# A Perceiver block on one Trainium2 core: the third norm's variance from sums, a second ring of split chunks, GpSimd without arithmetic behind attention, four loads issued earlier

## The chip, the cores and the metric

The kernel runs on one core of one Trainium2 chip, in float32, with 256 query tokens and 25088 context rows of width 2048. The metric is the device time of one execution in microseconds (us); lower is better. The kernel before was timed in three runs: 2530.39, 2532.25 and 2534.62 us, so the median is 2532.25 us.

## The reference

Three residual sub-blocks are computed. x is 256 x 2048, ctx is 25088 x 2048.

```
x = x + softmax(LN(x) @ ctx.T) @ ctx                         # cross attention over 25088 rows
q,k,v = LN(x) @ Wq, Wk, Wv + biases                          # 32 query heads, 8 key/value heads, DH 64
x = x + attention over the HEADS axis of each token          # scores[d,e] = sum_h q[d,h] k[e,h]
y = LN(x)
x = x + y @ W_base.T + b_base + sum_e route_e * (y @ A_e.T) @ B_e.T    # 8 experts, rank 16, top 2
```

In the second sub-block k and v are repeated four times along the head axis, so its output o, 256 x 2048 after the reshape, consists of 512 different columns, each four times in a row. LN is (x - mean) / sqrt(var + 1e-5) over the 2048 columns, without weights.

## The kernel before, in words

**Float32 by splitting.** A float32 product a*b runs on TensorE (PE) as three products of rounded halves (`product`, L1384 to L1386): hi*hi, hi*lo and lo*hi. The hi part is a cast on ScalarE (ACT), the lo part a subtraction of the hi part, on VectorE (DVE) or GpSimd (POOL).

**The long loop (up to 2200 us)** goes over 49 blocks of 512 context rows. The change leaves it alone. Behind it the k, q and v projections run on PE until 2304.8 us.

**Weights of the last product.** During the long loop W_base was turned into `wt_dram`, 64 pieces of 128 x 512 (4 output blocks `ob` times 16 input chunks), and its fourfold column sums into `wp_dram`, 16 such pieces (4 output blocks times 4 chunks). A piece is a "chunk" w, numbered 0 to 79: 0 to 63 multiply the x from before the second sub-block (`xt_hi`, `xt_lo`), 64 to 79 multiply the 512 columns of o. Since the third norm is linear once mean and variance are known, the kernel works out base(x1) and base(o) apart and scales both by ln3_a = 1/std at the end.

**The road of one chunk.** POOL issues its load into one of 4 buffers of `tr` (`load_base`, L636 to L648; it first waits until chunk w-4 is split). ACT casts it to `ch_hi` (`hi_base`, L836 to L840; it waits for the load and until PE has used chunk w-4, since `ch_hi` and `ch_lo` have 4 buffers too). The lo part is made on DVE (`lo_base`, L1193 to L1196) or on POOL (`lo_base`, L650 to L653): `by_pool(w)` gives POOL every fourth chunk below 64 and every second one from 64 on. Then PE does 6 matmuls of 512 columns (3 products for each of 2 token tiles). Every engine works strictly in the order in which the program lists its work, so whatever stands ahead of a wait delays what stands behind it.

**Chunks 0 to 15** run on PE behind the v projection, with small groups of transposes between (`A_AFTER`, `GATE_AFTER`, `SUM_AFTER`, `GSUM_AFTER`, `V_AFTER`). On ACT the drain of such a group stands behind the cast of the chunk four further on. Chunks 0 to 3 are loaded early (L656), but on POOL chunk 3's split and the loads from chunk 4 on stand behind `pool.wait_ge(qkv_done, 3 * TT)` at L682, which is the end of the v projection, and behind three memsets of `v_t`. Meanwhile the SP queue stores the split queries (`qk_dram`), reads them back in another layout (`q_t`, 12 transfers) and loads the broadcast bias `b_base_all` (1 MB).

**Attention** is a loop of 16 steps (`o`) on all engines, three chunks a step: scores (L1551), maximum and subtraction on DVE (L1229, L1233), exponent on ACT (L881), transposes on PE (L1412), the product with v (L1605). `keep_base` (ACT L848, DVE L1205) saves an output block's PSUM into `base_x` after every 16th chunk.

**Behind attention (from 2452 us).** PE does `router_chunks` (16 chunks of 136 columns, x1 times expert A and gate), in three parts, 0 to 6, 6 to 12 and 12 to 16. Between the last two it transposes the normalised attention output; ACT writes it as `o_nat` with its sums, DVE centres it (`oc_nat`), PE transposes that (`G_OC`), and PE multiplies it with the router's column sums (the "sum products") and with chunks 64 to 79 (`sum_chunks(ob)`, 24 matmuls each). DVE has one list of work here: `x2_tile(t)` adds o to x1 in `acc` (L1298), `x2_variance(t)` takes its statistics (L1303), ACT takes the root (`deviation`, L729), `factors` makes ln3_a (L995 to L999), then come the router's logits, softmax, top 2 and `hw` (up to L1351), with splits of chunks in between. `hw` is transposed on PE (L1686), copied by ACT (L959), and `experts_out(ob)` (L1677, a full float32 matmul of 2 passes) closes each output block. PE's order is sum_chunks 0, 1, 2, the transposes of hw, experts_out 0, sum_chunks 3, experts_out 1, 2, 3. POOL meanwhile splits half of the chunks and adds the bias to x2 in 8 pieces of 128 x 512 (`X2B_AFTER`, L700). At the end DVE adds `base_x` (`with_base`, L1362) and the PSUM sums (`result`, L1369), 8 passes each, and SP stores the 8 output pieces.

```
            for w in range(RING_TR, ALL_W + 3):
                if w < ALL_W:
                    load_base(w)
                if by_pool(w - 3):
                    lo_base(w - 3)
```

## Time and profile before

| what | value |
|---|---|
| median of three runs | 2532.25 us (2530.39 to 2534.62) |
| the profiled execution's own time | 2524.54 us |
| its span in the profile | 2522.9 us |
| busy PE, DVE, POOL, ACT | 2453.0, 1954.9, 1431.9, 1093.3 us |
| mean granted TensorE clock | 0.993 of full |

Busy times are sums over the span; a busy PE is not one at its peak, since its matmuls overlap in the records. Times such as "2482.91" are us from the start of the span. The timeline gives start, duration, engine, line, operation and, in brackets, how long the engine sat idle before it and what released it. The chain that ended last follows each piece of work back to what released it.

### The profile page before, as it was taken

The numbers are of one execution on the slowest core, as the hardware profiler recorded it, in microseconds if no ns is written. First come the engines' busy times: TensorE is split into PE (matmuls) and PEld (weight loads), VectorE is DVE, ScalarE is ACT, GpSimd is POOL, SyncE is SP. The second block draws the span as 40 slices with busy tenths as digits, with TensorE's granted clock in tenths as the row PEclk, the third lists the DMA queues.
The fourth block names the chain that finished last, engine by engine and source line by source line (L and its number), as shares of the span: only waits on it lengthen the run. The fifth ranks groups of instructions, "written<-read, shape, count | busy, mean of one in ns | idle before, by whom it ended". The sixth has DMA issues, their size and how long they took to land.

```text
span 2522.9 us, 36094 instructions
## 1 busy us (share of the span) xinstructions
PE 2453.0 (97%) x11446; PEld 2007.1 (80%) x11446; DVE 1954.9 (77%) x2693; ACT 1093.3 (43%) x1576; POOL 1431.9 (57%) x1064
## 2 busy tenths in 40 slices
PE   5999999999999999999999999999999999998997
PEld 4788888888888888888888888888888888876775
...
GB/s 236 216 224 206 228 207 231 219 204 226 207 229 226 211 216 212 218 219 209 222 217 202 219 218 220 213 218 212 205 219 220 217 215 211 213 160 145 146 112 67
DMA packets 421111, 518.22 MB, mean 205 GB/s; under 512 B 54406, under 2 KB 296070, under 8 KB 418440
## 3 DMA queue, kind: packets, MB, share of 16 engines
...
## 4 chain that ended last, share of the span: by engine, by line
PE 92%; DVE 4%; DMA 2%; SPq 1%; ACT 1%; issue 1%; POOL 0%; DVEq 0%; ACTq 0%; POOLq 0%
PE ps L1384 30%; PE ps L1386 30%; PE ps L1385 30%; PE ps L1393 2%; DMA tr<-wt_dram 1%; DVE ch_lo L1031 1%; DMA raw<-in_ctx_dram 1%; SPq L406 1%; DVE top_f L1339 0%; PE ps L1605 0%; PE ps L1551 0%; PE ps L1412 0%; DVE tr L1027 0%; DVE acc L1151 0%; PE ps L1677 0%
## 5 line engine op out<-in xcount | busy, mean ns | idle before, releaser
L585 POOL TENSOR_TENSOR nat_lo<-raw,nat_hi 128x512 fp32r<-128x512 f32 x784 | 1170.5, 1523 | 874.6 <-ACT nat_hi L738 842.1
L1031 DVE TENSOR_TENSOR ch_lo<-tr,ch_hi 128x512 fp32r<-128x512 f32 x784 | 849.9, 1084 | 369.0 <-ACT ch_hi L727 368.9
L727 ACT CAST ch_hi<-tr 128x512 fp32r<-128x512 f32 x784 | 477.2, 621 | 808.1 <-PE ps L1386 800.1
L1384 PE MATMUL ps<-ch_hi,xt_hi 128*128 128x512 f32 x1696 | 677.5, 399 | 14.9 <-DVE ch_lo L1031 9.9
L1386 PE MATMUL ps<-ch_hi,xt_lo 128*128 128x512 f32 x1696 | 663.3, 391 | 0.0
L1385 PE MATMUL ps<-ch_lo,xt_hi 128*128 128x512 f32 x1696 | 662.1, 390 | 0.0
L1384 PE MATMUL ps<-nat_hi,pt_hi 128*128 128x512 f32 x1568 | 611.8, 390 | 3.7 <-DVE pt_lo L980 3.7
L1386 PE MATMUL ps<-nat_hi,pt_lo 128*128 128x512 f32 x1568 | 610.3, 389 | 0.0
L1385 PE MATMUL ps<-nat_lo,pt_hi 128*128 128x512 f32 x1568 | 610.1, 389 | 0.0
L1027 DVE STREAM_TRANSPOSE tr<-quart 128x512 f32<-128x512 f32 x784 | 546.8, 698 | 0.0
L738 ACT CAST nat_hi<-raw 128x2048 fp32r<-128x2048 f32 x196 | 374.5, 1911 | 208.9 <-PE ps L1386 194.4
L1384 PEld LDWEIGHTS ps<-ch_hi,xt_hi 128*128 128x128 f32 x1696 | 319.3, 188 | 83.4 <-DVE ch_lo L1031 11.4
L1386 PEld LDWEIGHTS ps<-ch_hi,xt_lo 128*128 128x128 f32 x1696 | 319.0, 188 | 68.5
L1385 PEld LDWEIGHTS ps<-ch_lo,xt_hi 128*128 128x128 f32 x1696 | 319.6, 188 | 61.7
L1384 PEld LDWEIGHTS ps<-nat_hi,pt_hi 128*128 128x128 f32 x1568 | 294.3, 188 | 69.0 <-DVE pt_lo L980 4.4
L1386 PEld LDWEIGHTS ps<-nat_hi,pt_lo 128*128 128x128 f32 x1568 | 294.4, 188 | 61.4
L1385 PEld LDWEIGHTS ps<-nat_lo,pt_hi 128*128 128x128 f32 x1568 | 294.4, 188 | 60.7
L1069 DVE SCALAR_TENSOR_TENSOR acc<-acc,alpha,ps 128x512 f32<-128x512 f32 x248 | 177.7, 716 | 26.7 <-PE ps L1386 25.7
L711 ACT CAST pt_hi<-ps 128x512 fp32r<-128x512 f32 x98 | 57.2, 585 | 120.3 <-PE ps L1393 120.3
L1078 DVE SCALAR_TENSOR_TENSOR acc<-acc,alpha,ps 128x512 f32<-128x512 f32 x144 | 101.1, 702 | 4.9 <-PE ps L1386 4.9
L744 ACT ACTIVATE probs<-ps,neg_max 128x512 f32<-128x512 f32 x98 | 67.2, 686 | 77.5 <-DVE neg_max L1051 77.5
L1196 DVE TENSOR_TENSOR ch_lo<-tr,ch_hi 128x512 fp32r<-128x512 f32 x56 | 39.3, 710 | 71.9 <-ACT ch_hi L840 71.2
...
## 6 DMA issues: line engine op xcount, KB each, us to landing
...
```

The costliest lines, as they stand in the source:

```text
L585: last = pool.tensor_tensor(nat_lo[:, j, t], raw[:, j % 2, t], nat_hi[:, j, t].bitcast(F32), ALU.subtract)
L711: act.copy(dst, src).then_inc(hi_drained, 1)
L727: act.copy(ch_hi[:, c % RING_CH, :], tr[:, c % RING_TR, :]).then_inc(chunk_hi, 1)
L738: act.copy(nat_hi[:, j], raw[:, j % 2]).then_inc(nat_hi_ready, 1)
L744: act.activation(probs[:, q, :], ps[:, SCORE_BANK + TT * new + q, :], ACT.Exp, bias=neg_max[:, new, q:q + 1], accum_out=row_sum[:, q:q + 1 ...
L1027: dve.transpose(tr[:, c % RING_TR, :].rearrange("p (r i) -> p r i", i=SQ), src).then_inc(chunk_transposed, 1)
L1031: dve.tensor_tensor(ch_lo[:, c % RING_CH, :], tr[:, c % RING_TR, :], ch_hi[:, c % RING_CH, :].bitcast(F32), ALU.subtract).then_inc(chunk_s ...
L1069: dve.scalar_tensor_tensor(piece, piece, alpha[:, 1 - turn.parity, q:q + 1], ps[:, out_bank(v, turn.over), :], ALU.mult, ALU.add).then_inc ...
L1078: dve.scalar_tensor_tensor(piece, piece, alpha[:, turn.parity, q:q + 1], ps[:, out_bank(v, False), :], ALU.mult, ALU.add).then_inc(acc_upd ...
L1384: pe.matmul(out_, a_hi, b_hi, start=start, stop=False)
L1385: pe.matmul(out_, a_hi, b_lo, start=False, stop=False)
L1386: return pe.matmul(out_, a_lo, b_hi, start=False, stop=stop)
```

## The change

**Loads sooner.** POOL splits chunk 3 and issues loads 4 to 7 right behind the column sums of the expert weights, ahead of the wait for the v projection and the memsets.

**POOL's arithmetic behind attention is gone.** `by_pool(w)` is now only for chunks below 64, so DVE splits all of 64 to 79. The 8 bias additions move into the attention stage: one behind each of loads 22, 26, ... 50, and they add the bias to x1 (`acc` before o is added) into `x2_b`. DVE adds o later, into `x2_b`.

**Variance from sums.** With o repeated four times, var(x1 + o) = var(x1) + (2 * cross + square) / 2048, where cross = sum over 512 columns of (fourfold sum of x1 - 4 mean) * o and square = 4 * sum of (o - mean o)^2. DVE makes the fourfold sums of x1 (`x1_sum`, one `tensor_reduce` of 128 x 2048 to 128 x 512 a tile) in attention steps 10 and 11, and behind attention four `scalar_tensor_tensor` passes of 128 x 512 with an accumulated result, and two small ones. The second addition of 128 x 2048 a tile, its 8 `bn_stats` and 2 `bn_aggr` are no longer ahead of the factors; the additions themselves come behind `hw`.

**A second ring.** x1 (`acc`) isn't needed once bias additions and x1_sum are done. Its 16 KiB become `more_hi` and `more_lo`, 4 buffers each. Chunks 68 to 71 and 76 to 79 use them, so that from chunk 68 on a cast waits for chunk w-8 instead of w-4. ACT casts 68 to 71 and DVE splits them right at the end of attention, on DVE ahead of `att_norm(1)`.

**Orders.** PE: `router_chunks` in parts 0 to 4, 4 to 8, 8 to 14 (behind the transposes of attention's output) and 14 to 16 (behind the G_OC groups); sum_chunks 0, 1, 2, transposes of hw, experts_out 0 and 1, sum_chunks 3, experts_out 2 and 3. DVE and ACT: as in the diff.

```
     STEP_W = 3
+    MORE_W = BASE_W + RING_CH
     assert OCT * STEP_W == BASE_W - PRE_W
...
     def by_pool(w):
-        return w % 4 == 3 if w < BASE_W else w % 2 == 1
+        return w < BASE_W and w % 4 == 3
+    def users_before(w):
+        return w + 1 - (RING_CH if w < MORE_W else 2 * RING_CH)
...
         stages = (stage, sb("stage_b", [P, 4 * P]))
-        b_nat = sb("b_nat", [P, DC, ER])
-        acc = sb("acc", [P, TT, DIM])
+        at_b = room(8 * KIB)
+        b_nat = put(at_b, "b_nat", [P, DC, ER])
+        x1_sum = put(at_b, "x1_sum", [P, TT, QKC])
+        scrap = put(at_b + 4 * KIB, "scrap", [P, TT, QKC])
+        at_acc = room(16 * KIB)
+        acc = put(at_acc, "acc", [P, TT, DIM])
+        more_hi = put(at_acc, "more_hi", [P, RING_CH, KB], F32R)
+        more_lo = put(at_acc + 8 * KIB, "more_lo", [P, RING_CH, KB], F32R)
         xt_hi = sb("xt_hi", [P, DC, TOK], F32R)
...
         att_t = put(at_lo, "att_t", [P, 4, 4, P])
+        scrap2 = put(at_lo, "scrap2", [P, TT, QKC])
         o_norm = put(at_lo + 8 * KIB, "o_norm", [P, KVH, P])
...
                 pool.wait_ge(chunk_hi, DC * NB + w + 1)
-                pool.tensor_tensor(ch_lo[:, w % RING_CH, :], tr[:, w % RING_TR, :], ch_hi[:, w % RING_CH, :].bitcast(F32),
+                pool.tensor_tensor(w_lo(w), tr[:, w % RING_TR, :], w_hi(w).bitcast(F32),
                                    ALU.subtract).then_inc(pool_split, 1)
...
+            lo_base(3)
+            for w in range(RING_TR, 2 * RING_TR):
+                load_base(w)
             pool.wait_ge(qkv_done, 3 * TT)
...
             pool.wait_ge(v_zeroed, 3)
-            for w in range(RING_TR, ALL_W + 3):
-                if w < ALL_W:
-                    load_base(w)
+            def add_bias(piece):
+                t, cols = piece // FB, slice(piece % FB * KB, (piece % FB + 1) * KB)
+                if piece == 0:
+                    pool.wait_ge(bias_loaded, 4 * 16)
+                    pool.wait_ge(group_done, G_GSUM + 1)
+                pool.tensor_tensor(x2_b[:, t, cols], acc[:, t, cols], b_base_all[:, cols], ALU.add).then_inc(x1b_ready, 1)
+            for w in range(2 * RING_TR, ALL_W):
+                load_base(w)
                 if by_pool(w - 3):
                     lo_base(w - 3)
-                for piece in X2B_AFTER.get(w - 3 - BASE_W, ()):
-                    t, ob = piece // FB, piece % FB
-                    cols = slice(ob * KB, (ob + 1) * KB)
-                    if ob == 0:
-                        pool.wait_ge(x2_ready, t + 1)
-                    if piece == 0:
-                        pool.wait_ge(bias_loaded, 4 * 16)
-                    pool.tensor_tensor(x2_b[:, t, cols], acc[:, t, cols], b_base_all[:, cols], ALU.add).then_inc(x2b_ready, 1)
+                if w in BIAS_AFTER:
+                    add_bias(BIAS_AFTER[w])
...
                 act.wait_ge(base_loaded[w % RING_TR], 16 * (w // RING_TR + 1))
-                act.wait_ge(chunk_used, DC * NB + w + 1 - RING_CH)
-                act.copy(ch_hi[:, w % RING_CH, :], tr[:, w % RING_TR, :]).then_inc(chunk_hi, 1)
+                act.wait_ge(chunk_used, DC * NB + users_before(w))
+                if w == MORE_W:
+                    act.wait_ge(x1b_ready, TT * FB)
+                    act.wait_ge(x1_summed, TT)
+                act.copy(w_hi(w), tr[:, w % RING_TR, :]).then_inc(chunk_hi, 1)
...
             act.activation(warm[:, 0:1], ones[:, 0:1], ACT.Sqrt)
+            for w in range(MORE_W, MORE_W + RING_CH):
+                hi_base(w)
...
                 act.activation(router_x[:, t, :], ps[:, t, 0:AG], ACT.Copy, scale=ln_b[:, t:t + 1]).then_inc(router_kept, 1)
-            def base_range(first, end_):
-                for w in range(BASE_W + first, BASE_W + end_):
-                    hi_base(w)
-            base_range(RING_CH, STD_AT)
             for t in range(TT):
...
             act.activation(warm[:, 1:2], ones[:, 0:1], ACT.Exp)
-            base_range(STD_AT, EXP_AT)
+            for w in range(MORE_W + RING_CH, MORE_W + RING_CH + EXP_AT):
+                hi_base(w)
             for t in range(TT):
...
                                accum_out=gate_s[:, t:t + 1]).then_inc(gate_exped, 1)
-            base_range(EXP_AT, FB * PC)
+            for w in range(MORE_W + RING_CH + EXP_AT, ALL_W):
+                hi_base(w)
             act.wait_ge(hwt_done, 1)
...
                     att_norm(0)
+                if o in SUM_AT:
+                    if o == SUM_AT[0]:
+                        dve.wait_ge(plain_done, H_B + DC // 4)
+                        dve.tensor_scalar(mean4[:, :], mean_var[:, :, 0], float(REP), None, ALU.mult)
+                    t = SUM_AT.index(o)
+                    dve.tensor_reduce(x1_sum[:, t, :], acc[:, t, :].rearrange("p (n j) -> p n j", j=REP), AX.X,
+                                      ALU.add).then_inc(x1_summed, 1)
+            for w in range(MORE_W, MORE_W + RING_CH):
+                lo_base(w)
             att_norm(1)
...
                                   o_mean[:, t:t + 1], None, ALU.subtract).then_inc(oc_ready, 1)
-            for t in range(TT):
+            def lo_oc(t):
                 lo_group(G_OC + t, oc_lo[:, :, t * P:(t + 1) * P], bank4(PLAIN_BANK + t), oc_hi[:, :, t * P:(t + 1) * P])
-            def x2_tile(t):
-                dst = acc[:, t, :].rearrange("p (n j) -> p n j", j=REP)
-                link(dve.tensor_tensor(dst, dst, o_nat[:, t, :].unsqueeze(2).broadcast_to([P, QKC, REP]), ALU.add))
-                dve.sem_inc(x2_ready, 1)
-            def x2_variance(t):
-                for i in range(4):
-                    last = dve.bn_stats(stats[:, t, i, :], acc[:, t, i * 512:(i + 1) * 512])
-                link(last)
-                variance(t)
+            dve.wait_ge(x1_summed, TT)
+            for t in range(TT):
+                dve.scalar_tensor_tensor(scrap[:, t], x1_sum[:, t], mean4[:, t:t + 1], o_nat[:, t], ALU.subtract, ALU.mult,
+                                         accum_out=cross[:, t:t + 1])
+                if t == 0:
+                    lo_oc(0)
+            lo_oc(1)
+            dve.wait_ge(oc_ready, TT)
+            for t in range(TT):
+                last = dve.scalar_tensor_tensor(scrap2[:, t], oc_nat[:, t], float(REP), oc_nat[:, t], ALU.mult, ALU.mult,
+                                                accum_out=square[:, t:t + 1])
+            link(last)
+            link(dve.scalar_tensor_tensor(shift[:, :], cross[:, :], 2.0, square[:, :], ALU.mult, ALU.add))
+            dve.scalar_tensor_tensor(var3[:, :], shift[:, :], 1.0 / DIM, var_eps[:, :], ALU.mult, ALU.add).then_inc(var_ready, TT)
...
-            x2_tile(0)
-            x2_variance(0)
-            lo_sum(4)
-            x2_tile(1)
-            lo_sum(6)
-            x2_variance(1)
+            def x2_tile(t):
+                dst = x2_b[:, t, :].rearrange("p (n j) -> p n j", j=REP)
+                dve.wait_ge(x1b_ready, TT * FB)
+                link(dve.tensor_tensor(dst, dst, o_nat[:, t, :].unsqueeze(2).broadcast_to([P, QKC, REP]), ALU.add))
             lo_sum(8)
-            factors(2, slice(0, TT), 1, ln3_a, ln3_b)
+            factors(2, slice(0, TT), 1, ln3_a, ln3_b, of=var3)
...
             dve.tensor_reduce(gate_m[:, :], lg[:, :, :], AX.X, ALU.max, negate=True).then_inc(gate_max, 1)
-            lo_sum(10)
+            lo_sum(9)
             dve.wait_ge(gate_exped, TT)
...
             link(last)
+            lo_sum(10)
             dve.tensor_copy(top_f[:, :, :], top_i[:, :, 0:2])
...
                                   ALU.mult).then_inc(hw_ready, 1)
+            lo_sum(11)
+            x2_tile(0)
             lo_sum(12)
-            lo_sum(14)
+            x2_tile(1)
+            lo_sum(13)
...
                     piece = slice(ob * KB, (ob + 1) * KB)
-                    dve.wait_ge(x2b_ready, FB * t + ob + 1)
                     link(dve.scalar_tensor_tensor(x2_b[:, t, piece], base_x[:, t, piece], ln3_a[:, t:t + 1], x2_b[:, t, piece],
...
-            for ob in range(FB):
-                with_base(ob)
-                if ob:
-                    result(ob - 1)
-            result(FB - 1)
+            with_base(0)
+            lo_sum(14)
+            with_base(1)
+            lo_sum(15)
+            result(0)
+            with_base(2)
+            result(1)
+            with_base(3)
+            result(2)
+            result(3)
...
                 if o == OCT:
-                    router_chunks(0, 6)
-            router_chunks(6, 12)
+                    router_chunks(0, 4)
+            router_chunks(4, 8)
             pe.wait_ge(att_normed, 4)
...
                     last.then_inc(att_back, 1)
-            router_chunks(12, DC)
+            router_chunks(8, 14)
             pe.wait_ge(plain_drained, h_att(OCT - 1) + 1)
...
                 group(G_OC + t, PLAIN_BANK + t, [chunk_cols(oc_nat[:, t], c) for c in range(PC)], back=t + 1)
+            router_chunks(14, DC)
...
             experts_out(0)
+            experts_out(1)
             sum_chunks(3)
-            for ob in range(1, FB):
-                experts_out(ob)
+            experts_out(2)
+            experts_out(3)
...
 TURN_AFTER = {(0, 8): 0, (0, 12): 1, (0, 16): 2, (1, 4): 3, (1, 14): 4}
-X2B_AFTER = {7: (0, 1), 9: (2, 3), 11: (4, 5), 13: (6, 7)}
-STD_AT = 8
-EXP_AT = 11
+BIAS_AFTER = {22 + 4 * i: i for i in range(8)}
+SUM_AT = (10, 11)
+EXP_AT = 2
...
```

## Rows read from the trace of the kernel before

**Rows 1.** The page, the chain that ended last, shares by line.
```profile
PE ps L1384 30%; PE ps L1386 30%; PE ps L1385 30%; PE ps L1393 2%; DMA tr<-wt_dram 1%; DVE ch_lo L1031 1%; DMA raw<-in_ctx_dram 1%; SPq L406 1%; DVE top_f L1339 0%; PE ps L1605 0%; PE ps L1551 0%; PE ps L1412 0%; DVE tr L1027 0%; DVE acc L1151 0%; PE ps L1677 0%
```

**Rows 2.** Busy time by stage: stretch, length, PE, PEld, DVE, ACT, POOL, clock, DMA.
```profile
2304.00:2350.00 46.00, 33.41 (x189) 26.16 (x187) 13.92 (x23) 18.62 (x34) 18.12 (x27) 0.89 0.69 166
2350.00:2452.00 102.00, 98.02 (x834) 74.99 (x834) 48.10 (x74) 51.49 (x89) 43.41 (x62) 1.00 0.39 129
2452.00:2522.90 70.90, 52.54 (x266) 39.27 (x266) 48.32 (x77) 15.24 (x36) 23.94 (x24) 0.84 0.20 65
```

**Rows 3.** Waits in 2300 to 2352: total us, times, longest.
```profile
ACT ch_hi L840 <- DMA tr<-wt_dram: 25.3, 9, 8.2
```

**Rows 4.** Tile tr, loads issued from 2312 to 2316.5.
```profile
DMA to landing us min/median/max: 14.0/16.1/19.2
```

**Rows 5.** Tile tr, loads issued from 2350 to 2400.
```profile
DMA to landing us min/median/max: 2.8/2.8/4.4
```

**Rows 6.** Busy time and DMA share around the queries' return.
```profile
2285.00:2305.00 20.00, 20.00 (x90) 16.57 (x89) 3.79 (x5) 1.22 (x2) 4.52 (x6) 1.00 0.59 102
...
2315.00:2325.00 10.00, 3.23 (x16) 2.38 (x15) 0.69 (x1) 0.62 (x1) 0.54 (x1) 0.88 0.99 176
```

**Rows 7.** Timeline of the SP queue: store and return of the queries.
```profile
2288.59 16.29 SPq L536 DMA_DIRECT2D qk_dram<-q_nat  x2
2310.39 5.03 SPq L544 DMA_DIRECT2D q_t<-qk_dram  x12
```

**Rows 8.** Timeline of ACT, the cast of chunk 11 and the first base_x.
```profile
2337.53 0.62 ACT L840 CAST ch_hi<-tr 128x512 fp32r<-128x512 f32 x1 [1.09 <-DMA tr<-wt_dram]
...
2349.88 0.69 ACT L848 ACTIVATE base_x<-ps,ln_b 128x512 f32<-128x512 f32 x1
```

**Rows 9.** Timeline inside attention: a GpSimd load, its cast, a DVE gap.
```profile
2410.85 0.55 POOL L648 DMA_DIRECT2D tr<-wt_dram  x1 [0.30 <-POOL ch_lo L653]
...
2417.01 0.60 ACT L840 CAST ch_hi<-tr 128x512 fp32r<-128x512 f32 x1
...
2420.72 0.69 DVE L1196 TENSOR_TENSOR ch_lo<-tr,ch_hi 128x512 fp32r<-128x512 f32 x1 [3.01 <-ACT ch_hi L840]
```

**Rows 10.** Timeline of DVE behind attention.
```profile
2466.67 2.28 DVE L1298 TENSOR_TENSOR acc<-acc,o_nat 128x2048 f32<-128x2048 f32 x1
...
2476.48 2.46 DVE L1303 BATCH_NORM_STATS2 stats<-acc 128x6 f32<-128x512 f32 x4
...
2482.91 4.13 DVE L998 TENSOR_SCALAR ln_b<-ln_a 128x2 f32<-128x2 f32 x1
...
2490.22 9.51 DVE L1339 CAST top_f<-top_i 128x4 f32<-128x4 uint32 x1
...
2501.34 0.49 DVE L1351 TENSOR_TENSOR hw<-router_u,route 128x128 f32<-128x128 f32 x2
...
2502.95 3.10 DVE L1362 SCALAR_TENSOR_TENSOR x_b<-base_x,ln_a,x_b 128x512 f32<-128x512 f32 x4
...
2516.38 2.73 DVE L1369 SCALAR_TENSOR_TENSOR x_b<-ps,ln_a,x_b 128x512 f32<-128x512 f32 x4
```

**Rows 11.** Timeline of POOL behind attention.
```profile
2484.49 2.52 POOL L700 TENSOR_TENSOR x_b<-acc,b_base_all 128x512 f32<-128x512 f32 x2
...
2498.45 1.25 POOL L653 TENSOR_TENSOR ch_lo<-tr,ch_hi 128x512 fp32r<-128x512 f32 x1
```

**Rows 12.** Timeline of PE behind attention.
```profile
2461.45 0.31 PE L1384 MATMUL ps<-ag_hi,xt_hi 128*128 128x136 f32 x1
...
2464.17 1.24 PE L1393 MATMUL ps<-ident,oc_nat 128*128 128x128 f32 x8
...
2501.89 0.69 PE L1686 MATMUL ps<-ident,hw 128*128 128x128 f32 x2 [7.09 <-DVE hw L1351]
...
2506.99 0.39 PE L1385 MATMUL ps<-ch_lo,oc_hi 128*128 128x512 f32 x1
...
2512.23 5.31 PE L1677 MATMUL ps<-b_t,hw_t 128*128 128x512 f32 x12
```

27 lines of the change are left out of this document (18 added, 9 removed).

## The prediction

> **What bounds the kernel now.** I read the page first, then the busy time by stage, then the waits and timelines of the stages that the change touches. In the chain that ended last, 90% is the three lines of `product` on PE [rows 1], and nearly all of that lies in the long loop, which the change leaves alone. What can move is the last 219 us. Busy time by stage [rows 2] shows three different states. In 2304 to 2350 PE is busy 33.4 of 46.0 us at a clock of 0.89. Inside attention it is busy 98.0 of 102.0 us: PE sets the pace there, and a gain on any other engine is worth nothing. Behind attention it is busy 52.5 of 70.9 us at 0.84, with DVE at 48.3.
>
> The first idle stretch is a matter of loads: ACT waited 25.3 us for the chunks' loads [rows 3]. The three loads issued between 2312 and 2316.5 needed 14.0 to 19.2 us to land [rows 4], where one inside attention needs 2.8 [rows 5]. In that stretch the queries come back: q_t is issued from 2310.4 to 2315.4 [rows 7], and the DMA engines are 99% busy in 2315 to 2325, against 59% in 2285 to 2305 [rows 6].
>
> The second is DVE's list. Two instructions of two and four columns stand out: L998 took 4.13 us and ended at 2487.04, L1339 took 9.51 us and ended at 2499.73 [rows 10]. GpSimd's bias pair ended at 2487.01 and its last split at 2499.70 [rows 11], 0.03 us before each. So each stood until a run of GpSimd arithmetic was over. PE then waited 7.09 us for `hw` [rows 12].
>
> **Part 1, loads sooner.** Chunk 3's split and loads 4 to 7 are issued by POOL near 2293, where DMA is 59% busy and PE full [rows 6]; they land before the v projection ends. From then on chunk w stands where w-4 stood: chunk 15 finds what chunk 11 found. Chunk 11 was cast at 2337.5 [rows 8], and with POOL's split (1.3) was ready at 2339.5. Chunk 15's six matmuls (0.23 apart, 1.4) then end at 2340.9; now they end at about 2349.2, since the base_x copy behind them starts at 2349.88 [rows 8]. That is 8.3 us. Against it stands one effect: the four loads, 1 MB, now share the engines with the store of the queries, issued at 2288.6, on whose end the q_t reads wait (they began at 2310.4 [rows 7]). I put that at 1.3 us, less than half of one undisturbed landing of 2.8. I take -7. The bounds: at best all of PE's idle time (46.0 - 33.4 = 12.6 us) and some 3 us of the slow clock, -15; at worst the reads are late by four loads' share and nothing is gained, 0 to +3. What is late next: the landing of q_t, which is hidden today.
>
> **Part 2, attention.** Added are 8 bias additions on POOL (2.52 for two, 1.26 each [rows 11]) and on DVE two sums over 128x2048. The nearest row for the latter is L1298, 2.28 for the same number of elements [rows 10]; half of it or twice it is possible. Behind each addition a load is later by 1.26 us. Chunk 43 shows the cover: load issued 2410.85, landing 2.8 later, 2413.65, while its cast began at 2417.01 [rows 5, 9]. 3.4 us of slack covers 1.26. DVE was busy 48.1 of 102 us [rows 2] and had gaps such as the 3.01 us ahead of 2420.72 [rows 9]; a split that is 2.3 us late has three chunks of PE (4.2 us) before it is needed. I take 0. If the cover failed every time: 8 x 1.26 + 2 x 2.3 = 15 us. The moved splits 65 and 67 cost something at the very end: DVE copies its half of base_x behind split 67 instead of ahead of it, so that PE's first router chunk is late by about 0.4.
>
> **Part 3, PE behind attention.** (a) Eight router chunks instead of twelve stand ahead of the back-transposes. Chunk 12 to 15 ran from 2461.45 to 2464.17 [rows 12], 0.68 each. Four of them are 2.7 us; less 0.4 from above and without idle time otherwise, the transposes end near 2459.1 instead of 2461.45. DVE must have `att_norm(1)` done by 2458.2, behind four splits; by the casts' and splits' 0.6 to 0.7 each I estimate 2458.1 for it. (b) Six router chunks follow (4.1): the G_OC transposes start at 2463.2 instead of 2464.17, the other two router chunks cover ACT's cast and DVE's oc_lo, the sum products run 2465.5 to 2468.2. (c) Sum chunks 0 to 2 are 72 matmuls of 0.228 (23 of them from 2506.99 to 2512.23 [rows 12]), 16.5 us without a wait if every split is there: 2484.8. (d) Transposes of hw, ACT's copy: 2501.89 to the first expert matmul, 1.15; 2486.0. (e) experts_out: 12 passes in 5.31 [rows 12], 1.77 for an output block. Two, then 24 matmuls (5.5), then two: 2498.6.
>
> **Part 4, DVE behind attention.** oc_lo ends at 2466.4; the two squares are passes of 128x512, as L1362's 3.10 for four [rows 10], 0.78 each: 2468.0. From the end of tile 1's statistics (2478.94) to L998 (2482.91) it was 4.0 us [rows 10]: root, Exp table, one cast, one split, small steps. The same again, one root more: 2472.2. From L998's end (2487.04) to L1339's start, 3.2 us, and with one split more (0.7), 2476.2. From L1339's end to hw's (2501.83), 2.1: hw at 2478.5, 6.3 us before PE is ready for it. So DVE isn't what PE waits for, and the four second-ring chunks cover the way there: splits 72 to 75 are ready at about 2471.8, 2474, 2476 and 2479.2, and PE wants them from 2479.3 on. Behind hw DVE has 5 splits (3.5), two additions of o (4.6, moved, not removed) and 16 passes (12.4): 2499.0 by its own list, 2499.5 by PE's last block. Last pass before: 2516.38 + 2.73 = 2519.11 [rows 10]. Difference -19.6.
>
> In this sum the 13.3 us of the two stalls (9.36 + 3.97) and what leaves the way to the factors (2 x 2.28 + 2 x 2.46 = 9.5) don't simply add up: PE's own work catches up first, which is why it is 19.6 and not 23. The accumulating passes have no row; between 0.78 and twice that, four of them cost 0 to 3 us more on DVE, and hw's lead of 6.3 takes it.
>
> What the stalls were matters for the price. The rows show each of them ending with a whole run of GpSimd work, L1339's with a run that held the last four bias additions. The Trainium skill, "SBUF — State Buffer", "Who interferes with whom", says that such a DVE instruction and a GpSimd instruction exclude each other and that the later one waits until the first is finished. By that rule alone each stall would be about one GpSimd instruction; the trace disagrees in length (9.51 us, several instructions), not in the culprit.
>
> **The sum.** -7 - 19.6 + 0 = -26.6, 1.1% of the span. Against the profiled execution's 2524.54 us that gives 2498. The three runs stand higher, at a median of 2532.25, 7.7 above the profiled one, and the long loop in which that difference must lie is not touched, so I predict 2532.3 - 26.6 = 2506 (rounded) for the median.
>
> **The rivals.**
> (A) Forecast, both gains: 2506. Chance 0.60.
> (B) The start isn't gained: q_t lands when it lands, or the early loads delay it, and pair_scores(0) behind chunk 14 waits. For it: 99% busy DMA in 2315 to 2325 [rows 6]. Against it: PE now gets there only at 2347, long after. Only the tail gains: 2532.3 - 19.6 = 2513. 0.18.
> (C) The DVE stalls are only partly GpSimd's: each owes it one instruction (1.26 to 1.3), and the rest is the instruction's own. Then 2.5 us go and 10.8 stay. Then hw is ready at 2478.5 + 10.8 = 2489.3, PE has idled 4.5 us and runs its first expert block at half clock as now, the last pass ends near 2507, 12.5 are gained, with part 1 19.5: 2513. Against it: both ends coincide with GpSimd's to 0.03 us. 0.06. This is how it would come out by the Trainium skill's rule of one instruction, taken literally.
> (D) Attention loses part of what the ends gain, 5 to 15 us, through additions and sums that aren't covered: 2511 to 2521. 0.11.
> (E) Slower. Place: the load queue in attention. With an addition behind the split, POOL's next load is late, its cast, its split, and through the ring of four the load after it, so that PE goes at the pace of the loads over chunks 22 to 53. To end 5 us above before it must cost 32 us, 1.0 for each of these 32 chunks. It decides where addition and its waits hold POOL for more than 3.4 us, the slack at 2417.01 [rows 9]; the addition has 1.26. Then 2538. 0.03.
> (F) The change does nothing measurable, because the gains of the tail are eaten by D in full: 2532. 0.02.
>
> **Numbers.** A measurement of this kernel tells a change from none at about 0.2%, 5 us. Faster: A to D, 0.95; within 0.2%: F, 0.02; slower: E, 0.03. The range, 2497 to 2519: the lower end is A with part 1 near its best (-15) or runs that lie as low as the profiled one; the upper end holds B, C and two thirds of D.
>
> **What would show it.** In the profile after: loads 4 to 7 issued near 2293 and landed by 2306; chunk 15's end near 2341; attention still 98 of 102 us busy; L998 and L1339 at 0.2 us each; back-transposes 2.4 us sooner relative to attention's end; no PE wait above 0.5 us between the sum products and the transposes of hw, and a clock of 1.00 there; from attention's end to the span's end 51 us instead of 71. I am wrong if PE idles ahead of the first scores for more than 3 us (B), if a small DVE instruction stays above 1 us (C), or if attention takes more than 104 us (D, E).

## The result and the profile after

The changed kernel takes 2507.12 us (median of four runs, 2506.24 to 2509.8), the kernel before beside it 2533.43 (four runs, 2530.39 to 2535.13): ratio 0.9907, 95% interval 0.9892 to 0.9922. 2506 was predicted. A second set on another chip (`a_again` below) gave 0.9926 [0.9911, 0.9941], 19.3 us instead of 26.3. The profiled execution of the changed kernel took 2506.24 us with a span of 2504.5; that of before 2524.54. So from profile to profile only 18.3 us went.

To place them I cut each trace in three: the **start stretch** from POOL's first memset of `v_t` (the end of the v projection) to ACT's first `base_x`, **attention** from there to ACT's last `base_x`, and the **tail** from there to the end of the span. Busy time in these three stretches, changed kernel (stretch, length, PE, PEld, DVE, ACT, POOL, clock, DMA share, GB/s), to be held against [rows 2]:

```profile
2306.18:2350.20 44.02, 33.02 (x184) 25.31 (x182) 12.79 (x21) 18.52 (x34) 14.07 (x20) 0.87 0.75 165
2350.20:2453.57 103.37, 99.64 (x824) 75.87 (x826) 55.58 (x79) 50.75 (x88) 51.44 (x69) 0.97 0.39 125
2453.57:2504.50 50.93, 45.85 (x280) 37.26 (x277) 36.54 (x83) 16.14 (x38) 4.83 (x9) 1.00 0.29 94
```

Cut the same way, the profile of before has 44.8, 101.2 and 71.8 us. The tail is 20.9 shorter; its DVE work fell from 48 to 36.5 us, its POOL work from 24 to 4.8, and its clock is 1.00 instead of 0.84 [rows 2]. The start stretch gained 0.8 and began 1.1 later (2306.18 against 2305.11), and attention took 2.2 more, most of it the slow clock at its beginning (0.97 over the stretch; 0.50 until 2354, with PE busy 0.97 of the 2 us from 2350). The page's chain that ended last, changed kernel, has no `top_f` any more, where [rows 1] had one:

```profile
PE ps L1435 30%; PE ps L1437 30%; PE ps L1436 29%; PE ps L1444 2%; DMA tr<-wt_dram 2%; DVE ch_lo L1061 1%; SPq L429 1%; DMA raw<-in_ctx_dram 1%; SPq L559 0%; DVE tr L1057 0%; PE ps L1656 0%; DVE nat_lo L1201 0%; PE ps L1729 0%; PE ps L1602 0%; PE ps L1463 0%
```

What came in, with less than half a per cent, is `SPq L559`, the store of the queries. Timeline of DVE behind attention, changed kernel, against [rows 10]:

```profile
2474.27 0.17 DVE L1028 TENSOR_SCALAR ln_b<-ln_a 128x2 f32<-128x2 f32 x1
...
2478.23 0.17 DVE L1383 CAST top_f<-top_i 128x4 f32<-128x4 uint32 x1
...
2480.05 0.49 DVE L1395 TENSOR_TENSOR hw<-router_u,route 128x128 f32<-128x128 f32 x2
...
2481.06 2.29 DVE L1357 TENSOR_TENSOR x_b<-x_b,o_nat 128x2048 f32<-128x2048 f32 x1
...
2498.00 3.26 DVE L1415 SCALAR_TENSOR_TENSOR x_b<-ps,ln_a,x_b 128x512 f32<-128x512 f32 x4 [0.98 <-PE ps L1729]
```

The two instructions that stood for 4.13 and 9.51 us take 0.17 each. `hw` is ready at 2480.5. Timeline of PE, same stretch, against [rows 12]:

```profile
2460.91 1.06 PE L1697 MATMUL ps<-ident,o_norm 128*128 128x128 f32 x8
...
2465.78 1.06 PE L1444 MATMUL ps<-ident,oc_nat 128*128 128x128 f32 x8
...
2467.97 0.28 PE L1435 MATMUL ps<-sum_hi,oc_hi 128*128 128x136 f32 x1
...
2487.03 0.38 PE L1738 MATMUL ps<-ident,hw 128*128 128x128 f32 x2
2487.87 3.70 PE L1729 MATMUL ps<-b_t,hw_t 128*128 128x512 f32 x8 [0.46 <-ACT hw_t L989]
```

PE takes `hw` 6.5 us after it is ready, where it waited 7.09 us for it before. PE's waits from 2440 to the end add up to 1.0 us: 0.5, 0.3 and 0.2.

The start stretch shows the opposite. Timeline of the SP queue, changed kernel, against [rows 7]:

```profile
2288.93 25.34 SPq L559 DMA_DIRECT2D qk_dram<-q_nat  x2
...
2319.64 4.47 SPq L567 DMA_DIRECT2D q_t<-qk_dram  x12
...
2324.16 0.36 SPq L580 DMA_DIRECT2D b_base_all<-in_L_ffn_b_base_dram  x1
```

Tile `tr`, its loads issued from 2292 to 2298 (the four early ones), and waits in 2300 to 2352 (total, times, longest), against [rows 3, 5]:

```profile
DMA to landing us min/median/max: 17.3/18.2/19.2
```
```profile
ACT ch_hi L872 <- DMA tr<-wt_dram: 22.9, 9, 9.3
...
PE ps L1435 <- DVE ch_lo L1226: 7.3, 1, 7.3
...
PE ps L1602 <- DMA q_t<-qk_dram: 2.1, 1, 2.1
```

The early loads needed some 18 us to land, not 3, and the queries' return was issued 9.25 us later than before (2319.64 against 2310.39). ACT waited for loads nearly as long as before (22.9 against 25.3), and PE now also waits for `q_t`. The casts of chunks 14 and 15 in the timeline of ACT, changed kernel:

```profile
2338.94 0.62 ACT L872 CAST ch_hi<-tr 128x512 fp32r<-128x512 f32 x1 [9.34 <-DMA tr<-wt_dram]
2342.61 0.62 ACT L872 CAST ch_hi<-tr 128x512 fp32r<-128x512 f32 x1 [3.05 <-DMA tr<-wt_dram]
```

Chunk 11 was cast 15.7 us sooner than before (2321.88 against 2337.53 [rows 8]) and chunk 13 some 12 us sooner (2326.51). Chunk 14's load then took the lead away again, and chunk 15 was cast when it had been cast before (2342.6 against 2342.8).

### The profile page after: what moved, and what is told of

Its sections match the earlier page's. It is cut to its first block, busy times and chain, and to the rows that moved or that the text cites. A ratio compares the mean times of both kernels' runs of the same rounds, so it can differ in the third digit from the quotient of the medians.

```text
span 2504.5 us, 36094 instructions
## 1 busy us (share of the span) xinstructions
PE 2453.2 (98%) x11446; PEld 2009.8 (80%) x11446; DVE 1948.7 (78%) x2702; ACT 1093.8 (44%) x1576; POOL 1420.5 (57%) x1056
## 4 chain that ended last, share of the span: by engine, by line
PE 92%; DVE 3%; DMA 2%; SPq 1%; ACT 1%; issue 0%; POOL 0%; ACTq 0%; POOLq 0%
PE ps L1435 30%; PE ps L1437 30%; PE ps L1436 29%; PE ps L1444 2%; DMA tr<-wt_dram 2%; DVE ch_lo L1061 1%; SPq L429 1%; DMA raw<-in_ctx_dram 1%; SPq L559 0%; DVE tr L1057 0%; PE ps L1656 0%; DVE nat_lo L1201 0%; PE ps L1729 0%; PE ps L1602 0%; PE ps L1463 0%
## 5 line engine op out<-in xcount | busy, mean ns | idle before, releaser
L1099 DVE SCALAR_TENSOR_TENSOR acc<-acc,alpha,ps 128x512 f32<-128x512 f32 x248 | 177.8, 717 | 26.5 <-PE ps L1437 25.6
L1108 DVE SCALAR_TENSOR_TENSOR acc<-acc,alpha,ps 128x512 f32<-128x512 f32 x144 | 101.2, 703 | 4.9 <-PE ps L1437 4.9
```

Of the source, the lines that this page charges most:

```text
L1099: dve.scalar_tensor_tensor(piece, piece, alpha[:, 1 - turn.parity, q:q + 1], ps[:, out_bank(v, turn.over), :], ALU.mult, ALU.add).then_inc ...
L1108: dve.scalar_tensor_tensor(piece, piece, alpha[:, turn.parity, q:q + 1], ps[:, out_bank(v, False), :], ALU.mult, ALU.add).then_inc(acc_upd ...
```

## The experiments

The ratios compare with runs of the kernel before on the same chip. `b_again`, `b_loads`, `a_oldloads` and `a_kwait` ran on one chip, `a_again`, `a_onering`, `b_quiet` and `a_pooltail` on a second, the three `c_` kernels on a third and `b_quietpad` on a fourth. Medians of different chips are compared through their ratios. The last three columns are the profiled execution's.

| kernel | median us (range), runs | ratio to before [95%] | start | attention | tail |
|---|---|---|---|---|---|
| before | 2533.43 (2530.39 to 2535.13), 4 | 1 | 44.8 | 101.2 | 71.8 |
| after | 2507.12 (2506.24 to 2509.8), 4 | 0.9907 [0.9892, 0.9922] | 44.0 | 103.4 | 50.9 |
| b_again | 2531.45 (2525.5 to 2535.77), 10 | 0.9994 [0.9976, 1.0013] | 54.6 | 101.2 | 72.2 |
| a_again | 2512.16 (2506.46 to 2514.6), 6 | 0.9926 [0.9911, 0.9941] | 47.6 | 101.2 | 55.8 |
| b_loads | 2530.6 (2525.9 to 2534.74), 10 | 0.9994 [0.9977, 1.001] | 43.2 | 103.2 | 71.6 |
| a_oldloads | 2514.52 (2508.52 to 2521.29), 5 | 0.9925 [0.99, 0.995] | 49.4 | 101.4 | 63.9 |
| a_kwait | 2513.29 (2508.03 to 2517.0), 5 | 0.9927 [0.9898, 0.9956] | 49.3 | 101.4 | 55.7 |
| a_onering | 2515.28 (2510.83 to 2518.08), 4 | 0.9947 [0.9929, 0.9964] | 43.2 | 103.5 | 55.3 |
| b_quiet | 2530.99 (2522.47 to 2537.94), 9 | 0.9999 [0.9982, 1.0015] | 46.1 | 101.2 | 75.1 |
| a_pooltail | 2512.87, one run | - | 42.8 | 101.8 | 60.7 |
| c_pairs | 2504.46 (2500.26 to 2508.64), 4 | 0.9897 [0.9881, 0.9912] | 43.9 | 101.3 | 51.0 |
| c_pad | 2504.63 (2502.96 to 2512.68), 5 | 0.9897 [0.9881, 0.9913] | 47.1 | 103.2 | 52.5 |
| c_padpairs | 2505.29 (2502.87 to 2507.37), 4 | 0.9893 [0.9878, 0.9908] | 44.8 | 101.3 | 52.5 |
| b_quietpad | 2521.48 (2518.07 to 2526.39), 7 | 0.9959 [0.9945, 0.9974] | 49.8 | 101.2 | 62.9 |

### Both kernels again: b_again, a_again

No edit.

> The kernel before, once more, unchanged. The gain in the medians was 26 us, the difference of the two profiled spans 18.4. If the one profiled execution of before was a low one by chance, this profile lies near 2530 and shows where the other 8 us are; if it lies near 2524 again, profiled and timed executions of before differ for another reason. The ratio to before should be 1.000, and its interval says what the measurement can tell.

> The changed kernel, once more, unchanged. The two variants of it in the job before came out at 2513 to 2515, and both profiles show a granted clock of about 0.6 behind attention while PE was busy without a gap; the changed kernel's one profile shows 1.00 there. Theory: the clock behind attention differs from execution to execution of any of these kernels, and that is what separates 2514 from 2507: then this job gives the changed kernel a median of 2508 to 2514 and a spread of 8 us or more. Rival: the early loads themselves are worth 7 us: then 2507 again, spread under 4 us.

Busy time in the three stretches of `b_again`, then in the first two of `a_again`:

```profile
2304.36:2358.93 54.57, 35.88 (x184) 28.12 (x182) 14.17 (x24) 18.34 (x33) 18.07 (x26) 0.78 0.70 141
2358.93:2460.12 101.19, 97.42 (x824) 74.52 (x826) 47.42 (x73) 50.69 (x88) 42.73 (x61) 1.00 0.38 126
2460.12:2532.30 72.18, 51.66 (x280) 38.61 (x277) 48.47 (x78) 16.15 (x38) 24.67 (x24) 0.89 0.20 66
```
```profile
2306.31:2353.94 47.63, 33.62 (x184) 26.06 (x182) 14.49 (x24) 18.70 (x34) 14.65 (x21) 0.79 0.72 148
2353.94:2455.12 101.18, 97.42 (x824) 74.51 (x826) 54.05 (x76) 50.68 (x87) 51.05 (x68) 1.00 0.37 125
```

The first profile of before was a short one: its span is 9.4 us under `b_again`'s, and 9.8 of it lies in the start stretch (44.8 against 54.6), none in the long loop. In `a_again` attention takes 101.2 us with the 8 additions and 2 sums in it, as before without them. Its median is the 2508 to 2514 that had been expected, with a spread of 8.1 us. Its tail took 4.9 us more than in the first profile, with the clock low (below).

### The loads alone: b_loads, a_oldloads, a_kwait

`b_loads` is the kernel before with part 1; `a_oldloads` the changed kernel without it; in `a_kwait` the early loads also wait until the keys have been read back.

```
# b_loads (before)                        # a_oldloads (after): the reverse
             sums(a_nat, a_sum, ...)
+            lo_base(3)
+            for w in range(RING_TR, 2 * RING_TR):
+                load_base(w)
...
-            for w in range(RING_TR, ALL_W + 3):
+            for w in range(2 * RING_TR, ALL_W + 3):
# a_kwait (after)
             lo_base(3)
+            pool.wait_ge(k_back, 16 * TT * len(K_PARTS))
             for w in range(RING_TR, 2 * RING_TR):
```
(`k_back` is a new semaphore that the keys' read-back raises; the queries' read-back keeps `qk_back`.)

> The kernel before with part 1 alone: chunk 3's split and loads 4 to 7 issued ahead of the wait for the v projection. Theory: the early loads share the DMA engines with the read-back of the keys and the store of the queries, so that q_t is issued some 9 us later (2319 to 2320 instead of 2310), later loads fall into q_t's reads, and nothing is gained: the time within 2 us of before, and PE waits for q_t. Rival: part 1 gains its 7 us, and what ate it in the changed kernel is something else: then about 2525 in the median.

> The changed kernel with loads 4 to 7 and chunk 3's split back behind the memsets; all else as changed. Theory: within 2 us of the changed kernel (2507), q_t issued near 2310 again, and no slow clock at the start of attention. Rival (part 1 is worth 7 us): 2514.

> The changed kernel, but POOL waits for the read-back of the keys (a semaphore of its own) before it issues loads 4 to 7. Theory: the four loads no longer slow the keys' read-back; they are issued near 2303, land by about 2308, q_t is issued near 2311, and the first chunks are there when PE wants them: 3 to 8 us faster than the changed kernel, 2500 to 2504. Rival: q_t's own read-back holds all later loads whatever is done ahead of it, and the time stays within 2 us of 2507.

Timeline of the SP queue and a PE wait in 2300 to 2352, `b_loads`:

```profile
2288.60 23.62 SPq L536 DMA_DIRECT2D qk_dram<-q_nat  x2
...
2317.62 4.18 SPq L544 DMA_DIRECT2D q_t<-qk_dram  x12
```
```profile
PE ps L1555 <- DMA q_t<-qk_dram: 4.7, 1, 4.7
```

In the kernel before, part 1 alone changes nothing that can be measured (0.9994, as `b_again`; the interval's lower end, 0.9977, leaves at most 5.8 us for a gain). Taking it out of the changed kernel costs nothing that can be measured either (0.9925 against `a_again`'s 0.9926, on two chips). `a_oldloads` by itself came out at 2514.52, the rival's number and not the theory's 2507. But the changed kernel again gave 2512.16, and the profile of `a_oldloads` lost 13 us in the tail to the clock, which part 1 doesn't touch.

The reason why part 1 gains so little shows in the SP queue. From the issue of the queries' store to that of their return it took 21.6 to 24.8 us in the six profiles in which POOL's loads waited (before, `b_again`, `b_quiet`, `b_quietpad`, `a_oldloads`, `a_kwait`), and 29.0 to 30.9 in five of the six with early loads and unpaired transfers (23.2 in `a_again`). The loads find the engines busy with the store, and the store shares them with the loads. What ACT wins on chunks 4 to 7, the queries and the chunks behind them lose. Start and attention together took 144.7 to 150.3 us in the six with early loads, 146.0 to 155.8 in five of the six without (`a_kwait` aside, whose memset itself began later). The means, 147.4 and 150.2, differ by 3 us, less than either set spreads.

Part of the price is paid in attention: in the five profiles in which the queries came back late, PE waited 1.8 to 5.3 us for `q_t`, and attention took 103.2 to 103.5 us in four of them (`b_loads` among them; 101.8 in `a_pooltail`), 101.2 to 101.4 in all others. The loads that were held longest were issued beside the queries' return and the 1 MB bias behind it; which of the two held them wasn't separated.

In `a_kwait` the queries returned early (issued 2312.28), but its loads came late: PE stood 15.7 us for `ag_lo`, the drain of a transpose group, whose first half stands behind a chunk's cast on ACT. The wait bought nothing: 2513.29 instead of the 2500 to 2504 expected.

### Without the second ring: a_onering

```
-    MORE_W = BASE_W + RING_CH
+    MORE_W = ALL_W
```
(with it go the casts and splits of 68 to 71 at the end of attention; DVE does splits 68 to 71 ahead of the factors.)

> The changed kernel without the second ring: chunks 68 to 71 are cast and split behind the sum products, each once PE has used the chunk four before, in the one ring of four. Theory: DVE has 4 splits (2.8 us) more between var3 and the factors; hw is later by 3 to 4 us, still about when PE is ready for it (its lead was 6 us), and DVE's list behind hw ends 3 us later: 1 to 4 us slower than the changed kernel. Rival: PE waits for chunks as before, 6 us or more.

PE waits from 2453 on and timeline of DVE, `a_onering`:

```profile
PE ps L1723 <- ACT hw_t L984: 2.3, 1, 2.3
```
```profile
2485.63 0.49 DVE L1389 TENSOR_TENSOR hw<-router_u,route 128x128 f32<-128x128 f32 x2
```

`hw` begins 31.8 us after attention's end (2453.79) instead of 26.5, 5.4 later where 3 to 4 had been expected. PE waits for it again, and the tail is 4.4 us longer, at a clock of 1.00 for the same first 34 us. So by these two profiles the ring is worth 4.4 of the 20.9 us. The medians on the one chip differ by 3.1 us (2515.28 against `a_again`'s 2512.16), and their intervals overlap.

### GpSimd's arithmetic: b_quiet, a_pooltail

`b_quiet`: before, with POOL's splits behind attention given to DVE and the bias additions left out. `a_pooltail`: the changed kernel with seven GpSimd additions of 128 x 512 put back behind attention, three, two and two between POOL's last loads.

```
# b_quiet
-        return w % 4 == 3 if w < BASE_W else w % 2 == 1
+        return w < BASE_W and w % 4 == 3
# a_pooltail
+                if w == ALL_W - 5:
+                    pool.wait_ge(var_ready, 3 * TT)
+                for k in {ALL_W - 5: (0, 1, 2), ALL_W - 4: (3, 4), ALL_W - 3: (5, 6)}.get(w, ()):
+                    pool.tensor_tensor(extra[k // 4][:, k % 4, :], b_base_all[:, 0:KB], b_base_all[:, KB:2 * KB], ALU.add)
```

> The kernel before with GpSimd's arithmetic behind attention taken away alone: DVE splits all of chunks 64 to 79, and the bias additions are left out (the last pass reads x1 + o itself, the bias is not in the result). Variance by bn_stats, one ring, PE's order and the loads as before. Theory: the two small DVE instructions at L998 and L1339 fall from 4.13 and 9.51 us to 0.2, hw comes about 11 us sooner (13.3 less 3 more splits of 0.7), and since PE's chunks 72 to 75 must then be done first, the time falls by 9 to 12 us. Rival (those durations are their own, one GpSimd instruction each apart): 2 us or less.

> The changed kernel with seven GpSimd additions of 128x512 put in behind attention, into memory that nobody reads: three from the moment the variance is ready, two behind load 76, two behind load 77. Theory: the small DVE instructions of the factors and of the top-2 choice (L1028 and the cast at L1383, 0.17 us each) stall again until GpSimd pauses, one of them for over 3 us. Rival: none takes longer than one GpSimd addition, 1.3 us.

Timelines of POOL and of DVE, `a_pooltail`:

```profile
2472.51 4.24 POOL L734 TENSOR_TENSOR extra<-b_base_all 128x512 f32<-128x512 f32 x3 [14.52 <-DVE var L1354]
2476.69 0.56 POOL L672 DMA_DIRECT2D tr<-wp_dram  x1
2477.27 2.53 POOL L734 TENSOR_TENSOR extra<-b_base_all 128x512 f32<-128x512 f32 x2
```
```profile
2475.70 1.06 DVE L1031 TENSOR_TENSOR ln_b<-var,ln_a 128x2 f32<-128x2 f32 x1
2476.80 3.03 DVE L1032 TENSOR_TENSOR ln_a<-ln_b,std 128x2 f32<-128x2 f32 x1
...
2483.22 2.74 DVE L1231 TENSOR_TENSOR ch_lo<-tr,ch_hi 128x512 fp32r<-128x512 f32 x1
```

With GpSimd's additions back, the holds are back, on other instructions: two-column ones that take 0.16 without them (L1026 and L1027 of the changed kernel) took 1.06 and 3.03 us, each ending within 0.03 us of a run of GpSimd work. A split of 128 x 512, which takes 0.69 without them, took 2.74 beside the third run (2482.85 to 2485.39). L1028 and the cast of L1383, on which the theory had put the holds, were not held: no addition ran when they began. The clock was low for some 10 us in this profile, ahead of the additions, so its tail is to be held against `a_again`'s: 60.7 against 55.8, 4.9 us.

With the two in the kernel before that makes five holds. In three of them the VectorE instruction had begun first. In the timeline of POOL, kernel before, the runs that ended with L998 and L1339 [rows 10] begin 0.35 and 0.31 us after them:

```profile
2483.26 1.29 POOL L653 TENSOR_TENSOR ch_lo<-tr,ch_hi 128x512 fp32r<-128x512 f32 x1
...
2490.53 1.28 POOL L653 TENSOR_TENSOR ch_lo<-tr,ch_hi 128x512 fp32r<-128x512 f32 x1
```

In `a_pooltail` L1032 began 0.47 us ahead of its run. Each time GpSimd was issuing a load when the instruction began.

`b_quiet` puzzled. Its small instructions were as short as in the changed kernel:

```profile
2500.68 0.17 DVE L990 TENSOR_SCALAR ln_b<-ln_a 128x2 f32<-128x2 f32 x1
2504.39 0.17 DVE L1334 CAST top_f<-top_i 128x4 f32<-128x4 uint32 x1
```

Yet its median is no lower than that of before, where 9 to 12 us had been expected. Its busy time from 6 us behind attention's end on, then that of `a_again` in steps of 4 us from 1 us behind attention's end on:

```profile
2460.23:2488.23 28.00, 27.45 (x132) 26.11 (x132) 9.16 (x20) 4.44 (x13) 0.00 (x0) 0.50 0.00 1
```
```profile
2456.12:2460.12 4.00, 3.75 (x26) 3.48 (x25) 2.27 (x4) 3.20 (x6) 1.27 (x3) 0.75 0.22 76
2460.12:2464.12 4.00, 4.00 (x32) 3.96 (x31) 1.89 (x6) 0.62 (x1) 1.42 (x3) 0.50 0.66 231
2464.12:2468.12 4.00, 4.00 (x21) 4.00 (x20) 0.00 (x0) 0.77 (x3) 0.00 (x0) 0.50 0.09 33
2468.12:2472.12 4.00, 4.00 (x38) 4.00 (x36) 2.18 (x8) 1.36 (x6) 0.00 (x0) 0.97 0.01 2
```

In `b_quiet` PE is busy 27.45 of 28.00 us at a granted clock of 0.50, the 1.2 GHz level; in `a_again` it is at 0.50 for some 10 us. Timeline of PE behind attention's end (2454.23), `b_quiet`:

```profile
2454.96 0.33 PE L1378 MATMUL ps<-ag_hi,xt_hi 128*128 128x136 f32 x1 [0.34 <-ACT base_x L840]
...
2455.76 0.33 PE L1378 MATMUL ps<-ag_hi,xt_hi 128*128 128x136 f32 x1 [0.25 <-DVE base_x L1197]
```

The second of these two waits is new. In the kernel before POOL splits chunks 65 and 67 and PE waits once, 0.34 us; here and in the changed kernel DVE splits them first and copies its half of `base_x` later, so PE waits again.

The nine runs of `b_quiet` fall in two groups: three of 2522.47 to 2524.38 us with a mean clock of 0.993 or 0.994, six of 2529.65 to 2537.94 with 0.986 to 0.989. Against the median of before on this chip, 2531.44, the first three gain some 8 us; in the other six the clock takes that back.

### The queries' transfers and the width of the router's matmuls: c_pairs, c_pad, c_padpairs, b_quietpad

```
# c_pairs (after): two parts per transfer, 8 for the queries, 10 for the keys
-Q_PARTS = (0, 0, 1, 1, 0, 2)
-K_PARTS = (0, 1, 0, 1, 2, 0)
+Q_PARTS = (0, 1, 0, 1, 0, 2)
+K_PARTS = (0, 1, 1, 0, 2, 0)
...
-                        sp.dma_start(to[at:at + KVH], qk_dram[w, part, :, t * P:(t + 1) * P]).then_inc(qk_back, 16)
+                        sp.dma_start(to[at:at + KVH * n],
+                                     qk_dram[w, parts[k]:parts[k] + n, :, t * P:(t + 1) * P].rearrange("s g m d -> (s g) m d")
+                                     ).then_inc(qk_back, 16)
# c_pad (after), b_quietpad (b_quiet): 272 columns, the second 136 never read
+            def two(of, c):
+                return of[:, c:c + 2, :].rearrange("p c n -> p (c n)") if c + 1 < of.shape[1] else of[:, c, :]
...
-                        last = product(t, x_part(xt_hi, c, t), x_part(xt_lo, c, t), ag_hi[:, c, :], ag_lo[:, c, :],
+                        last = product(t, x_part(xt_hi, c, t), x_part(xt_lo, c, t), two(ag_hi, c), two(ag_lo, c),
```
(and the same for the sum products; `c_padpairs` has both edits.)

> The changed kernel with the parts of the queries and keys read back in another order, so that two parts go in one transfer: 8 transfers in place of 12 for the queries, 10 in place of 12 for the keys. Theory L (the start stretch is set by the transfers between the queries' store and the first scores, and TensorE waits for the last of them): from the issue of the queries' store to that of the table that ends SyncE's queue it takes 2 to 5 us less than in the changed kernel, the stretch from the early loads to ScalarE's first cast of attention 2 to 5 us less than its 44 to 47.6, and the median of the runs falls from about 2510 to 2505 to 2508. Rival M (the engines are as full as before, since the bytes are the same; the stretch only swings by itself): the stretch stays in 43 to 50 us and the median within 2 us of the changed kernel's 2507 to 2512. Behind attention nothing differs between the two theories.

> The changed kernel with the router's and the sum product's matmuls 272 columns wide in place of 136 (this chunk's and the next one's columns; the second half of the result is never read), so that TensorE streams more columns in each while the stretch behind attention runs. Theory C (the granted clock falls behind attention in about every second execution, although TensorE is busy there without a gap, because its matmuls are so narrow): the clock stays at 1.00 from attention's end to the end of the span; the wider matmuls cost 1 to 6 us there by themselves, so that the stretch takes 52 to 57 us, but the runs lie closer together, within 4 us but for the start stretch, and the median is 2507 to 2513. Rival D (the clock falls for another reason than the matmuls' width): it falls in this kernel as well, the stretch takes 56 to 70 us, and the median is 2513 to 2520.

> Both edits together. Theories L and C: start stretch 2 to 5 us shorter, clock 1.00 behind attention, median 2502 to 2509. If only one of them holds, the stretch that it is about shows it and the other one swings as in the changed kernel; if neither, the median is 2513 or more.

> The kernel before with GpSimd's arithmetic behind attention given to VectorE (the bias is left out of the result, as in b_quiet) and with the router's and the sum product's matmuls 272 columns wide in place of 136. b_quiet had the same without the wide matmuls: three of its runs took 2522.5 to 2524.4 us and six took 2529.7 to 2537.9, and in the profiled one the granted clock was 0.5 for some 34 us behind attention. Theory C (GpSimd's stalls cost before about 10 us, and narrow matmuls lose the clock once the stalls are gone): the clock stays at 1.00 behind attention until the result's waits, the stretch from attention's end to the span's end takes 61 to 66 us in place of 71.8 and 75.1, all runs lie within 2518 to 2528 and the median is 2520 to 2525 (ratio 0.995 to 0.998). Rival D (the width has nothing to do with it): the runs spread over 2522 to 2538 again, with a median of 2527 to 2532. Rival S (the stalls cost before nothing, whatever the clock): clock 1.00, and the stretch still takes 70 us or more.

**Pairs.** Timeline of the SP queue in `c_pairs`, then in `c_padpairs`:

```profile
2284.95 20.04 SPq L559 DMA_DIRECT2D qk_dram<-q_nat  x2
2310.46 3.77 SPq L569 DMA_DIRECT2D q_t<-qk_dram  x8
```
```profile
2288.79 19.41 SPq L559 DMA_DIRECT2D qk_dram<-q_nat  x2
2312.57 3.09 SPq L569 DMA_DIRECT2D q_t<-qk_dram  x8
```

From store to return it took 25.5 and 23.8 us, against 30.7, 23.2 and 30.3 in `after`, `a_again` and `c_pad`, and the early loads landed after 12.7 and 13.0 us (median), there after 18.2, 13.4 and 18.7. Since `a_again` has the short values without pairs, two profiles don't show that the pairs made them. The start stretch, at 43.9 and 44.8 us, is no shorter than the changed kernel's 44.0: that expectation missed. PE then waited for a chunk's split instead (5.2 and 10.1 us). Both medians lie 2 to 3 us under the changed kernel's first, but so does that of `c_pad`, which ran on the same chip without pairs (2504.63). So a gain isn't shown.

**Width.** Busy time over the tail of `c_pad`, then of `b_quietpad`:

```profile
2456.86:2509.40 52.54, 47.51 (x280) 38.77 (x277) 36.52 (x83) 16.24 (x38) 4.83 (x9) 0.99 0.28 91
```
```profile
2454.70:2517.60 62.90, 51.18 (x280) 40.48 (x276) 39.21 (x85) 16.10 (x38) 4.83 (x9) 0.94 0.23 76
```

The padding costs 1.6 us (52.5 against 50.9). The first 34 us behind attention were at 1.00 in all three profiles with it. Without it, in the eight profiles in which DVE splits chunks 65 and 67, the clock fell 3.0 to 3.8 us behind attention's end in five (`a_again`, `a_oldloads`, `a_kwait`, `a_pooltail`, `b_quiet`) and held in three (`after`, `a_onering`, `c_pairs`). In the three profiles in which POOL splits them (before, `b_again`, `b_loads`) it held there. On the chip of the three `c_` kernels it held in the one profile without the padding as well as in the two with it, and the medians are the same (2504.46, 2504.63, 2505.29). `c_pad` missed what was expected of it: 2507 to 2513, with runs within 4 us but for the start; its runs spread over 9.7 us, and the profiled one, at 2511.2, has 47.1 us in the start stretch. `c_padpairs` lay in its 2502 to 2509.

In the changed kernel, then, the padding gains nothing that these runs can show. In `b_quiet` it does: `b_quietpad`'s seven runs have a mean clock of 0.992 to 0.995, where six of `b_quiet`'s nine were under 0.990, and against before on its own chip the ratio is 0.9959 [0.9945, 0.9974] where `b_quiet` has 0.9999 [0.9982, 1.0015]. All of its runs and its median came as expected (2518 to 2528, 2520 to 2525). The two kernels ran on different chips. The padding also shortens PE's second wait, from 0.25 to some 0.15 us. So it isn't shown whether the width, that wait or the chip kept the clock up; a kernel with narrow matmuls and without the second wait wasn't run.

**What the parts of the tail are worth.** GpSimd's arithmetic alone is worth 71.8 - 62.9 = 8.9 us in `b_quietpad`, or some 10.5 if the padding's 1.6 are taken off; the ring is worth 4.4. The variance from sums and PE's order were not run by themselves. If the parts add up, which isn't shown, some 6 us of the 20.9 are left for both together (an estimate from these profiles).

## Why the prediction was right, and where it wasn't

**Parts 3 and 4, the tail: right in size and in its steps.** The forecast's times hold from the old attention's end (2451.08); the changed kernel's came 2.5 us later. Less those 2.5: transposes done by 2459.2 (forecast 2459.1), G_OC from 2463.3 (2463.2), sum products 2465.5 to 2468.2 (the same), hw transposed from 2484.5 (2484.8), factors at 2471.8 (2472.2), hw at 2478.05 (2478.5) with a lead of 6.5 (6.3), last pass at 2498.8 (2499.5). To the last pass that is a gain of 20.3, forecast 19.6; to the end of the span it is 20.9. The accumulating passes, which had no row, took 0.68 to 0.75 us and 0.08 or 0.09 to read the sum: the cheap end of their bounds.

**Part 2, attention: right about what it added.** 101.2 us with the additions and sums (`a_again`) and 101.2 without. One sum took 2.28 us, as the row taken for it. D and E didn't come. The 2.2 us that attention took more in `after` are part 1's: the late queries, the wait for them and the slow clock behind it, and `b_loads`, which has part 1 alone, shows them too (103.2).

**Part 1, the start: wrong.** The step that failed is "they land before the v projection ends. From then on chunk w stands where w-4 stood". It priced the landing by a row from inside attention (2.8) and the queries' delay at less than half of one such landing (1.3). The loads took 17.3 to 19.2 us and landed between 2310 and 2314, behind the v projection's end and not by 2306; the queries came back 9.25 us later. Even where they did land by about 2308 (`a_again`, 13.3 to 13.7 us), chunk 15 didn't find what chunk 11 had found: the wait for a slow load moved on to a later chunk (chunk 14 in `after`), and PE stood 8.7 us for a split. Chunk 15 was cast at 2342.6, as before. The sign of rival B was more than 3 us of PE idle ahead of the first scores: PE waited 2.1 us for `q_t` in `after`, 4.7 in `b_loads`, 5.3 in `c_pad`, so `after` itself stayed under it. Landings of 14 to 19 us stood in [rows 4], in the same stretch of the same queues, and I left them out as something that the change would avoid. The two comparisons of medians show no gain from part 1 (`b_loads` leaves at most 5.8 us), the means of the profiles some 3 us, which is within their spread; 7 was forecast. The DMA share in 2285 to 2305 went from 0.59 [rows 6] to 0.80. The trace agrees here with the Trainium skill, "DMA: Bandwidth & Descriptors", "Issuing engines are not separate DMA queues": transfers run on the same 16 engines and interleave, whoever issues them.

**The anchor: wrong as argued.** "The long loop in which that difference must lie": by the one other profile of before, it lay in the start stretch (44.8 against 54.6 us in `b_again`). I had read the row of a lucky stretch and taken its differences off a median that holds less lucky ones.

**The total: met in part by luck.** 2506 was met by 2507.12, with a part 1 that was sized some 4 to 7 us too large. The medians differ by 26.3, and the tail gives 20.9 of it; the other 5.4 have no row, and the start stretch swings by 10 us from one execution to the next. The second set, 19.3 us of gain and 2512.16, has rival B's number, 2513, but not B's terms: the tail of its profile gained only 16.0, since the clock fell, and its start and attention lay 7 us under those of `b_again` and 2.8 over those of the first profile. Both sets lie in the range 2497 to 2519. Between forecast and B they don't decide, and the experiments on part 1 speak for B's mechanism.

**Rival C** is refuted: the held instructions fell to 0.17 us each, `b_quiet` shows the same with the other parts of the change left out, so all 13.3 us of them were GpSimd's, and `a_pooltail` brought such holds back. The rule of one instruction by the Trainium skill, "SBUF — State Buffer", "Who interferes with whom", falls short again, in length and in order: L1032 was held through a run of two GpSimd additions that began 0.47 us after it did, though the same section gives the ports to whoever issues first. That is, the holds are shown to be GpSimd's; why they last for a whole run isn't.

**Not foreseen** was the clock behind attention. In all three profiles with POOL's splits the tail's first 28 us were at full clock; the changed kernel loses it there in some executions, and with it 5 us (`a_again`) to 13 us (`a_oldloads`, 63.9). The loss begins at 3 to 4 us, where no stall had ever been (the first of the two came 32 us behind attention's end), so it isn't the stalls' absence that brings it. What does differ there is what part 2 priced at 0.4 us and no more: DVE's later copy of `base_x` and PE's second wait. Whether that wait brings the loss wasn't tested.
